# Second attention of a two-layer kernel: keys from the back, maxima two units ahead, causal masks on Pool

## What is computed

```
q, k, v = split(x @ w_qkv)            # x: layer norm of the residual; B=2, S=1024, D=128
q, k = rope(q), rope(k)               # H=16 heads, dh=8
scores = einsum('bhqd,bhkd->bhqk', q, k) * dh ** -0.5
scores = where(tril, scores, -huge)   # causal
attn = softmax(scores)
out = einsum('bhqk,bhkd->bhqd', attn, v) @ w_out
```

## Time and profile before

| | |
|---|---|
| median of 3 runs | 993.67 us (993.42 to 994.7) |
| profiled execution | 993.18 us |
| its span, first to last instruction | 991.3 us |
| busy over the span: PE, PEld | 849.9 (86%), 505.0 (51%) |
| busy: DVE, ACT, POOL | 595.4 (60%), 516.4 (52%), 329.3 (33%) |
| mean granted clock of TensorE | 0.92 |
| second attention, first scores to last values | 621.4 to 938.5 |

### The profile page before, as it was taken

One profiled execution on the slowest core, in us unless ns is written; L12 is line 12 of the kernel. 1 busy time (PEld: TensorE's weight loads), 2 busy tenths in 40 slices (PEclk: granted clock), 3 DMA queues, 4 the chain that ended last, 5 costly groups with the idle time before them and its releaser, 6 DMA issues.

```text
span 991.3 us, 15069 instructions
## 1 busy us (share of the span) xinstructions
PE 849.9 (86%) x5146; PEld 505.0 (51%) x5146; DVE 595.4 (60%) x1294; ACT 516.4 (52%) x875; POOL 329.3 (33%) x332
## 2 busy tenths in 40 slices
PE   5899999988999865899998435899999999999858
PEld 2454444343343233479987323555555555555435
DVE  6867776767666157553357598557575575754051
ACT  3246566564565642336665211656656566565632
POOL 3327666655566861660140840110202102000000
PEclk9779999998999996799999566899999999999969
DMA  9300000000000000112230200000000000000001
GB/s 330 123 1 1 1 1 1 1 1 1 1 1 1 1 1 0 59 59 62 70 97 29 84 3 1 1 1 1 1 2 1 1 0 0 0 1 1 1 1 43
DMA packets 22634, 24.38 MB, mean 25 GB/s; under 512 B 3591, under 2 KB 20105, under 8 KB 22314
## 3 DMA queue, kind: packets, MB, share of 16 engines
q1 hardware_dynamic: 19896, 17.90, 5.5%
q0 software_dynamic: 2048, 4.20, 1.5%
q10 hardware_dynamic: 626, 1.43, 0.4%
HBM read 14.34 MB, written 9.18 MB: 24 GB/s over the span
## 4 chain that ended last, share of the span: by engine, by line
PE 62%; DVE 23%; ACT 7%; issue 5%; POOL 2%; DMA 1%; ACTq 0%; DVEq 0%; SPq 0%; POOLq 0%
PE ps L1348 8%; PE ps L1400 6%; PE ps L1032 6%; PE ps L1024 5%; PE ps L1001 5%; DVE mx_part L2021 5%; PE ps L1374 4%; DVE mx_part L1631 3%; ACT rounded L613 3%; PE ps L1040 3%; PE ps L1291 3%; DVE cT L1654 2%; PE ps L990 2%; PE ps L1202 2%; ACT pt L851 2%
## 5 line engine op out<-in xcount | busy, mean ns | idle before, releaser
L1631 DVE TENSOR_REDUCE mx_part<-ps 128x1 f32<-128x512 f32 x256 | 162.5, 681 | 70.6 <-PE ps L1001 69.8
L851 ACT ACTIVATE pt<-ps 128x1024 f32<-128x1024 f32 (+1 forms) x160 | 142.8, 938 | 86.7 <-PE ps L1374 45.7
L670 ACT ACTIVATE pt<-ps 128x512 f32<-128x512 f32 x256 | 139.9, 596 | 80.3 <-PE ps L1024 78.2
L2021 DVE TENSOR_REDUCE mx_part<-ps 128x1 f32<-128x512 f32 (+3 forms) x256 | 138.9, 586 | 37.7 <-PE ps L1352 23.9
L1348 PE MATMUL ps<-rounded 128*128 128x512 f32 (+3 forms) x384 | 143.1, 426 | 12.2 <-DVE mx_part L2021 4.5
L613 ACT ACTIVATE rounded<-ps 32x512 fp32r<-32x512 f32 (+3 forms) x166 | 98.2, 593 | 100.9 <-PE ps L1327 32.2
L1024 PE MATMUL ps<-rounded 100*128 100x512 f32 x256 | 121.0, 484 | 8.5 <-ACT pt L670 7.8
L1001 PE MATMUL ps<-rounded 98*128 98x512 f32 x256 | 107.9, 444 | 17.4 <-DVE mx_part L1631 16.7
L1348 PEld LDWEIGHTS ps<-rounded 128*128 128x128 f32 x384 | 73.7, 203 | 76.2 <-DVE mx_part L2021 49.8
L1374 PE MATMUL ps<-rounded 128*128 128x512 f32 (+3 forms) x384 | 104.2, 370 | 8.9 <-ACT pt L851 7.2
L2021 DVE TENSOR_REDUCE mx<-ps 128x1 f32<-128x128 f32 (+3 forms) x128 | 57.2, 487 | 83.4 <-PE ps L1352 82.0
(11 more groups left out here) (249 smaller groups left out, 1285.9 us busy)
## 6 DMA issues: line engine op xcount, KB each, us to landing
wm<-in_wm SPq DMA_DIRECT2D x1, 4896.0 KB, 15.5
kstage<-to_experts SPq DMA_DIRECT2D x10, 256.0 KB, 3.4
of_experts<-pt SPq DMA_DIRECT2D x10, 256.0 KB, 2.3
to_experts<-kstage SPq DMA_DIRECT2D x4, 512.0 KB, 4.1
wm<-in_experts SPq DMA_DIRECT2D x1, 1028.0 KB
x<-in_x SPq DMA_DIRECT2D x4, 256.0 KB, 6.2
out<-x SPq DMA_DIRECT2D x4, 256.0 KB, 2.3
to_experts<-kstage SPq DMA_DIRECT2D x2, 448.0 KB, 4.4
```

Source lines behind the costliest of these rows:

```text
L670: nc.scalar.activation(pt0(k, i), ps[:, ST0_BANKS[i % 2], :], ACT.Exp, scale=SCALE0).then_inc(exp_done, 1)
L851: nc.scalar.activation(pt[:, 4 * (t % 2) + 2 * g:4 * (t % 2) + 2 * g + 2, 0:w], ps[:, ST1_BANKS[2 * g]:ST1_BANKS[2 * g] + 2, 0:w], ACT.Exp ...
L1631: v.tensor_reduce(mx_part[u % 2][:, o:o + 1], ps[:, max_bank(u, n), :], AX_X, ALU.max).then_inc(max_done, 1)
L2021: v.tensor_reduce(dst, ps[:, banks[s % len(banks)], o:o + w], AX_X, ALU.max).then_inc(max1_done, 1)
```

## The change

It touches the second attention only.

- **Order of keys and queries.** `ST1` now begins with the second half of the queries, and goes through the keys from the back: steps 0 to 2 are the diagonal tiles of the second half (4; 5 with 7; 6), steps 3 to 6 key tiles 3 to 0, steps 7 to 9 the diagonal tiles of the first half (0; 1 with 3; 2). The halves of a stack that are used up first are so free first.
- **Maxima.** `MX1` goes head by head, starts with the tiles of queries and keys of the second half, and the tiles run `MX1_AHEAD = 8` further ahead: in every step of unit `u` there are four, one behind the scores of each head; the last eight, in steps 8 and 9, belong to unit `u + 2`. Eight tiles of unit 1 come ahead of unit 0's first scores. The split of the maxima comes after step 7.
- **Stacks.** Keys are turned before queries, the second half before the first; ScalarE's four key copies are issued one by one between exponentials (`STACK1_KEYS`), and the counts of `stacked` follow (10 a unit). Turns: unit `u + 1`'s first halves in steps 0 and 2, unit `u + 2`'s second halves in steps 3 and 7, maxima both in step 9, contexts in steps 2 and 8, each turn in the middle of a step or at its end.
- **Masks.** The 32 bf16 matmuls a unit on the key-side scores go, and `mask_kq` with its load. Pool applies `affine_select` in place to the exponentials in `pt`: one instruction for each diagonal block of 128 keys and 128 queries over the 4 heads, 8 a unit. The values of a diagonal step wait for `masked1` in place of the exponentials.
- **Pool.** `stage` is cut in keys, queries and values; in each unit Pool stages the keys of `u + 2`, masks steps 0 to 2, stages the queries of `u + 2` and the values of `u + 1`, and masks steps 7 to 9.
- **Values.** The last values of a unit move behind step 0's scores of the next one.
- **Loops.** All eight units are straight code on every engine.

```diff
 ST1 = []
-for c in range(S // CH):
+for c in reversed(range(S // CH)):
     j0 = c * TC
-    ST1 += [(c, ((j, 0, CH),)) for j in range(j0 + 1)]
-    ST1 += [(c, ((j0 + 1, 0, CH - P), (j0 + 3, CH - P, P))), (c, ((j0 + 2, 0, CH - 2 * P),))]
+    own = [(c, ((j0, 0, CH),)), (c, ((j0 + 1, 0, CH - P), (j0 + 3, CH - P, P))), (c, ((j0 + 2, 0, CH - 2 * P),))]
+    ST1 += own + [(c, ((j, 0, CH),)) for j in reversed(range(j0))]
+DIAG1 = [[(o, w) for j, o, w in parts if j >= c * TC] for c, parts in ST1]
...
-for i0, c in ((0, 0), (TC, 0), (TC, 1)):
+for i0, c in ((TC, 1), (TC, 0), (0, 0)):
...
-    MX1 += [(r, c, p) for p in parts for r in range(HG)]
+    MX1 += [(r, c, p) for r in range(HG) for p in parts]
...
-MX1_STEP = (5, 5, 5, 5, 5, 5, 5, 5, 0, 0)
+MX1_AHEAD = 2 * HG
+MX1_SPLIT_STEP = K1 - 2
+NSTACK1 = 2 * (HG + 1)
+STACK1_KEYS = {0: (1, 1, 0), 1: (1, 1, 2), 4: (2, 0, 0), 5: (2, 0, 2)}
...
+            def mask(u, k):
+                if DIAG1[k]:
+                    pool.wait_ge(exp1_done, u * (2 * K1) + (2 * k + 2))
+                for o, w in DIAG1[k]:
+                    block = pt[:, 4 * (k % 2):4 * (k % 2) + HG, o:o + P]
+                    nc.gpsimd.affine_select(block, block, [[0, HG], [1, P]], ALU.is_ge, 0.0, base=0,
+                                            channel_multiplier=-1).then_inc(masked1, 1)
...
-            with pool.Fori(1, U1 // 2) as i:
-                for pp in range(2):
-                    stage(i * 2 + pp, pp, True)
+            for u in range(U1):
+                if u + 2 < U1:
...
+                    stage_keys(u + 2, u % 2)
+                for k in range(K1_FIRST):
+                    mask(u, k)
+                if u + 2 < U1:
+                    stage_queries(u + 2, u % 2)
+                if u and u + 1 < U1:
+                    stage_values(u + 1, 1 - u % 2)
+                for k in range(K1_FIRST, K1):
+                    mask(u, k)
...
             def unit1(u, pp, first=False, s=True, t=True):
                 for k in range(K1):
-                    exps1(u, k, first)
+                    for g in range(2):
+                        exps1(u, k, g, first)
+                        if k in STACK1_KEYS:
+                            du, n, r = STACK1_KEYS[k]
+                            if u + du < U1:
+                                stack_keys(u + du, (u + du) % 2, n, r + g)
+                        if k == 2 and g == 0 and s:
+                            stack_queries(u + 1, 1 - pp, 1)
+                        if k == 7 and g == 0 and t:
+                            stack_queries(u + 2, pp, 0)
+                        if k == K1 - 1 and s:
+                            max_rows1(u + 1, 1 - pp, g)
+                    if k == 0 and not first:
+                        context1_T(u - 1, 1)
                     if k == K1_FIRST:
-                        context1_T(u, 0, first)
+                        context1_T(u, 0)
...
                 elif not first:
-                    pe.wait_ge(max1_done, u * NMX1)
+                    pe.wait_ge(max1_done, (u - 1) * NMX1 + MX1_END[s - len(banks)])
...
-            def masks1(t):
-
-                c, parts = ST1[t]
-                if parts[0][0] < c * TC:
-                    return
-                for r in range(HG):
-                    for j, o, w in parts:
-                        ins = mm(ps[:, ST1_BANKS[r], o:o + P], identb[:], mask_kq[:], start=False,
-                                 stop=(o == parts[-1][1]))
-                    if r % 2:
-                        ins.then_inc(st1_mm, 1)
...
-                pe.wait_ge(exp1_done, u * (2 * K1) + (2 * t + 2))
+                if DIAG1[t]:
+                    pe.wait_ge(masked1, u * NDIAG1 + DIAG1_UPTO[t])
+                else:
+                    pe.wait_ge(exp1_done, u * (2 * K1) + (2 * t + 2))
...
                 for k in range(K1):
...
+                    for r in range(HG):
+                        scores1(u, pp, r, k, first)
+                        piece(k, r)
+                        if r != 1:
+                            continue
+                        if k == 0 and s:
+                            turn_stack(u + 1, 1 - pp, 2, (m1_rows, u * 2 + 2))
+                        if k == 2 and s:
+                            turn_stack(u + 1, 1 - pp, 3, (stacked, (u + 1) * NSTACK1 + (2 * HG + 1)))
+                        if k == 7 and t:
+                            turn_stack(u + 2, pp, 1, (stacked, (u + 2) * NSTACK1 + HG))
+                        if k == K1 - 1 and s:
+                            turn_max1(u + 1, 1 - pp, 0, (ctx1_out, u * 4 + 2))
                     if k:
                         values1(u, pp, k - 1, first)
...
+                    elif u:
+                        values1(u - 1, 1 - pp, K1 - 1, u == 1)
+                    if k == 2 and u:
+                        turn_context1(u - 1, 1, (stacked, (u + 2) * NSTACK1) if s else (m1_rows, u * 2 + 2))
+                    if k == 3 and t:
+                        turn_stack(u + 2, pp, 0, (ctx1_out, u * 4) if u else (stacked, (u + 2) * NSTACK1))
+                    if k == K1 - 2:
+                        turn_context1(u, 0, (stacked, (u + 2) * NSTACK1 + (HG + 1)) if t else (ctx1_out, u * 4))
+                    if k == K1 - 1 and s:
+                        turn_max1(u + 1, 1 - pp, 1, (m1_rows, u * 2 + 3))
...
+                if n == len(MX1) - 3:
+                    turn_stack(1, 1, 0, (qk_out, NT))
+            turn_max1(0, 0, 0, (stacked, NSTACK1 + HG))
+            turn_stack(1, 1, 1, (m1_rows, 1))
+            turn_max1(0, 0, 1, (stacked, NSTACK1 + (HG + 1)))
+            for n in range(MX1_AHEAD):
+                scores_max1(1, 1, n)
+            for u in range(U1):
+                unit1(u, u % 2, first=(u == 0), s=(u + 1 < U1), t=(u + 2 < U1))
+            values1(U1 - 1, (U1 - 1) % 2, K1 - 1, False)
```

More of the change, by code:

```diff
@@ L576, in stage, with stage_values @@
+            def stage_values(u, pp):
+                if u >= 2:
                     pool.wait_ge(pv1_mm, u * K1 - K1)
@@ L855, in context1_T, with stack_queries @@
-            def context1_T(u, c, first):
-                act.wait_ge(pv1_mm, u * K1 + (K1_FIRST if c == 0 else K1))
-                if not first:
-                    act.wait_ge(ctx1_turn, u * 2 + (c - 1))
-                copy(cT[:, c, :], ps[:, CTX_BANK, :]).then_inc(ctx1_T, 1)
+            def stack_queries(u, pp, n):
+                act.wait_ge(stack_turn, u * 4 + (2 * n + 2))
+                cols = slice((1 - n) * CH, (2 - n) * CH)
+                copy(query_stack1[pp][:, cols], ps[:, TURN1_BANK, :]).then_inc(stacked, 1)
@@ new lines, in stack_keys, with max_rows1 @@
+            def stack_keys(u, pp, n, r):
+                act.wait_ge(stack_turn, u * 4 + (2 * n + 1))
+                cols, rows = slice((1 - n) * CH, (2 - n) * CH), slice(RS * r, RS * (r + 1))
+                copy(key_stack1[pp][rows, r, cols], ps[rows, TURN1_BANK, :]).then_inc(stacked, 1)
+            def max_rows1(u, pp, n):
+                act.wait_ge(m1_turn, u * 2 + (n + 1))
+                copy(query_stack1[pp][:, (1 - n) * CH:(2 - n) * CH], ps[:, TURN1_BANK, :]).then_inc(m1_rows, 1)
@@ new lines, in exps1 @@
+            def exps1(u, t, g, first):
+                w = sum(m for _, _, m in ST1[t][1])
+                act.wait_ge(st1_mm, u * (2 * K1) + (2 * t + g + 1))
+                if not (first and t < 2):
+                    act.wait_ge(pv1_mm, u * K1 + (t - 1))
+                nc.scalar.activation(pt[:, 4 * (t % 2) + 2 * g:4 * (t % 2) + 2 * g + 2, 0:w],
+                                     ps[:, ST1_BANKS[2 * g]:ST1_BANKS[2 * g] + 2, 0:w], ACT.Exp,
+                                     scale=SCALE1).then_inc(exp1_done, 1)
@@ L880, in _ @@
                     front_qkv(c, t)
-            for hf in range(2):
-                max_rows1(0, 0, hf)
             act.wait_ge(keys_zero[1], 1)
-            for n in range(2):
-                stack(1, 1, n)
-            unit1(0, 0, first=True)
-            unit1(1, 1)
-            with act.Fori(1, U1 // 2 - 1) as i:
-                unit1(i * 2, 0)
-                unit1(i * 2 + 1, 1)
-            unit1(U1 - 2, 0, t=False)
-            unit1(U1 - 1, 1, s=False, t=False)
+            for r in range(HG):
+                stack_keys(1, 1, 0, r)
+            max_rows1(0, 0, 0)
+            stack_queries(1, 1, 0)
+            max_rows1(0, 0, 1)
+            for u in range(U1):
+                unit1(u, u % 2, first=(u == 0), s=(u + 1 < U1), t=(u + 2 < U1))
+            context1_T(U1 - 1, 1)
             for c in range(NCH):
@@ L1394, in values1 @@
                     pe.wait_ge(v_copied, u + 1)
-                if parts[0][0] == 0 and not (first and c == 0):
-                    pe.wait_ge(ctx1_T, u * 2 + c)
-                pe.wait_ge(exp1_done, u * (2 * K1) + (2 * t + 2))
+                if t == K1_FIRST or t == 0 and u:
+                    pe.wait_ge(ctx1_T, u * 2 + (1 - c))
+                if DIAG1[t]:
```

(25 more changed lines are left out.)

226 lines of the change are left out of this document (96 added, 130 removed).

## The result

The changed kernel takes 960.88 us (median of 4 runs, 958.83 to 964.08), the kernel before 993.54 (4 runs, 993.18 to 994.7): a ratio of 0.9672, 95% interval 0.9644 to 0.97. It is faster, by 32.7 us, where 23.0 were forecast. The profiled execution took 961.01 with a span of 959.2; that of before had a span of 991.3.

What follows compares the result with a forecast made beforehand. TensorE bounds the second attention, losing time to a two-bank ping-pong with VectorE. Gains of 2.3 (unit 0), 15.5 (units 1 to 5), 4.4 (unit 6) and 0.8 (unit 7) sum to 23.0: forecast 970.7 us, range 952 to 986.

Steps and rivals of the forecast that it cites:

- likeliest case: Whole kernel: the forecast itself, 970.7 us, with 965 to 977 counted as its case; chance 0.42.
- TensorE nearly full: Rival, second attention: first maximum overlaps better, loss only 4.3 a unit, unit 36.5, total 958 us; chance 0.20.
- Masks off TensorE: Each unit of the second attention: 32 key-side mask matmuls go, saving 1.5 us of TensorE's own time.
- A mask of 0.80: Pool, second attention: one mask block takes 0.80 us at the copy's rate for 512 elements, bounds 0.40 and 1.28.
- The loss of 6.0 a unit: Steady unit: TensorE loses 6.0 us beside own work of 32.3; unit 38.2, gain 3.1; loss before 7.5.
- Spread, stacks and maxima ahead: Steady unit: four tiles every step, earlier split and covered copies, all within the loss falling from 7.5 to 6.0 us.
- Unit 0: Start of second attention: scores at about 625.3, unit takes 38.2 less 0.9 plus 1.2, ends 663.8 not 666.13; gain 2.3 us.
- Unit 6: Second attention: lacks eight tiles (3.1) and two turns (0.7), waits 0.6 for a mask; 35.0 not 39.4, gain 4.4 us.
- Unit 7: Last unit, ScalarE's: loop through Pool's mask longer in diagonal steps, mask matmuls ahead of exponentials go; net gain 0.8 us.
- The slow mask: Rival: Pool's mask blocks delay values; slower than before from 1.65 us a block, 1028 us at 2.56; chance 0.12.
- Nothing overlooked: Denies the rival that wait order or straight-code delivery eats the gain, 0 to 10 us slower than before; chance 0.08.
- 0.4 for one instruction of the split: VectorE's split of maxima: one two-input instruction per unit could meet a Pool mask, costing 0.4 us that VectorE can spare.

Runs made afterwards that it cites:

- no_mask: Changed kernel without any key-side causal mask, values waiting for exponentials alone: 1000.6 us where the kernel before took 1033.74; steady unit 37.12, as in the changed kernel.
- pe_masks: Changed kernel with key-side masks back on TensorE, right behind each head's scores: ratio 0.983 to the kernel before; steady unit 39.05 us against 37.12.
- both_undone: Changed kernel with key-side masks on TensorE and maxima tiles five each in steps 0 to 7, none ahead of unit 0: 984.48 us, unit 40.74.
- mask_slow: Changed kernel with one clearing of an unused tile before each Pool mask, making a block 1.19 us: 1013.76 us, before 1033.74 there; unit 37.75.
- mask_slower: Changed kernel with two clearings of an unused tile before each Pool mask, making a block 1.86 us: 1031.66 us; unit 41.20 against 37.12.
- gaps: Changed kernel with each step's tiles 0 and 1 ahead of their scores, 2 and 3 behind: ratio 0.9664 to the kernel before; unit 36.77 us.

## Why the prediction was right, and where its sizes were off

The sign and the mechanism held: TensorE bound before and binds after, it gained by fewer matmuls and fewer waits for VectorE, and the mask lies beside it. The median of 960.9 is in the range of 952 to 986, but under the 965 to 977 of the likeliest case, and nearer to the rival "TensorE nearly full" (958) than to the forecast of 970.7; so is the unit, 37.1 beside 36.5 and 38.2. By its own steps:

- **Masks off TensorE, 1.5 a unit.** The mechanism was right; putting them back costs 1.9, since more than the masks' own pitches is lost.
- **A mask of 0.80.** It took 0.63. The copy's rate was an upper estimate, not a middle one. The margin of 1.8 was read rightly (1.87), and with no_mask the cover is shown. By the margin, an estimate from (1.87 - 0.1) / 2, a block of up to 0.9 costs a steady unit nothing.
- **The loss of 6.0 a unit.** This is the mis-sized term: own work of 32.3 and a unit of 37.12 leave 4.8. The gain of a steady unit is so 4.1 and not 3.1, and five of them make 5.2 of the 9.1 us that the sum fell short. By the prediction's own count per step, steps 1 to 4 (740.28 to 754.62) lost 2.6, where 3.4 stood. The full step shown lost 0.65, as VectorE started 0.43 after the matmul and not 0.5, and for the stack in step 2 TensorE waited 0.20 and not 0.4. The six other steps lost 2.3, where 2.6 stood. "TensorE nearly full" had 4.3 for the whole term and was nearer.
- **Spread, stacks and maxima ahead.** The prediction took the loss down from 7.5 to 6.0, and named a cover of 1.1 at the unit's boundary as a part of that; so it left 0.4 for the spread. The runs turn this around: the spread is worth 1.8, and all that is neither mask nor spread 0.54. So two errors that partly cancel stand behind the size of this term, and that it came out within 1.2 is in part luck.
- **Unit 0, 2.3.** The first scores came at 624.27 (forecast 625.3), the unit took 38.42 (38.5). The start, 1.0 earlier than forecast, is what the sum was short by.
- **Unit 6, 4.4.** 5.05: the same tiles' loss. The wait of 0.6 for a mask did not show; TensorE waited 0.53 for VectorE's context there instead.
- **Unit 7, 0.8.** It gained 2.3, and not by the step named. The prediction weighed mask matmuls that go against a longer loop through Pool and came to a net gain. The runs make it even: with the masks on TensorE the unit takes 24.5 (pe_masks), on Pool 24.4, with none 22.8 (no_mask). The 2.2 are there in both_undone too (24.5 against 26.7 before), so they belong to what that run keeps; which part of it is open. The price of 6 us per us of mask was high as well: mask_slow takes 26.9, 4.5 per us between a block of 0.63 and one of 1.19. Its diagonal values do wait for Pool, as forecast, on TensorE's timeline of the changed kernel:

```profile
888.99 1.05 PE L1425 MATMUL ps<-pt,v_cur 128*9 128x384 f32 x16 [0.79 <-POOL pt L597]
...
905.53 1.55 PE L1425 MATMUL ps<-pt,v_cur 128*9 128x384 f32 x24 [0.71 <-POOL pt L597]
```

- **The slow mask.** The rival's form was right: mask_slow cost what the margin says. In mask_slower its price was too low, as it left out the clock, but since the gain to eat was 32 and not 23, the break-even moved from 1.65 to some 1.8 to 1.9. Nothing like 12 cycles an element is in the 0.63 of a block of 512 (the Trainium skill, "GPSIMD Engine Reference", section 3.1, gives that for data-dependent branching): the select does not have that price. Its 1.2 ns an element lies between the 1.0 of the memset (0.63 for 640 columns, in mask_slow) and the 1.6 of the copy.
- **Nothing overlooked** in the order of waits: unit 1 and unit 3 are 37.11 and 37.12, and the second chip repeats 37.13.

What stays open: which part of the rest gave unit 0 and unit 7 their 2.2 us each in both_undone. The 0.65 behind the second attention needs no cause: over the fourteen traces, with the same code there, this stretch lies between 51.6 and 52.8.

## What to carry to other kernels

Where two engines hand two buffers to and fro, write down when each buffer is taken and freed in one step, for every kind of step, and place the filling engine's longest piece of other work right behind the filling of both. Work taken off the bound engine is free on an idle one exactly as long as it fits into the margin between its producer and its consumer: read that margin from the trace of before, and price what lies above it at one for one (mask_slow), and at more where the wait grows long enough to lower TensorE's clock (mask_slower). After each reordering look for the wait that comes up next; here the wait for one copy held back half of what the new order gave, until the turn was moved too.

## What the runs showed of the hardware

**The clock fell after a wait of 1.9 us.** In mask_slower TensorE waited 1.88 us and then ran at a granted clock of 0.55 over 2.60 us, mostly at the 1.2 GHz level, and at 1.00 (2.4 GHz) both ahead of it and from 797.00 on. Waits of 0.79 in the same place in unit 7 of the changed kernel, and of 0.67 in step 8 of the same unit of mask_slower, left the clock at 1.00. So 1.9 us of wait cost 1.9 + 1.5.

**A small VectorE instruction that starts beside a select lasts until the select ends.** VectorE's timeline of the changed kernel, the split of the maxima, with the mask of Pool that runs beside it:

```profile
765.68 0.18 DVE L2053 TENSOR_TENSOR mx<-mx_part 128x16 f32<-128x16 f32 x1
765.89 0.52 DVE L2058 TENSOR_SCALAR qstage<-mx 128x32 fp32r<-128x32 f32 x1
766.44 0.22 DVE L2060 SCALAR_TENSOR_TENSOR qstage<-mx,qstage 128x32 fp32r<-128x32 f32 x1
```

```profile
765.72 0.64 POOL L597 TENSOR_SCALAR_AFFINE_SELECT pt<-pt 128x512 f32<-128x512 f32 x1 [15.54 <-ACT pt L882]
```

The second instruction ends at 766.41, just after the select (766.36), and took 0.20 in before. It is so in the six of the changed kernel's eight splits in which it starts during a select (0.52 to 0.54); in the two others, and in all of no_mask, which has no selects, it took 0.20. The first instruction, which has two inputs and began 0.04 ahead of the select, was not held up. In the split of unit 7's maxima it began 0.23 behind the start of one (Pool's select from 876.50 to 877.13), and there it was:

```profile
876.73 0.43 DVE L2053 TENSOR_TENSOR mx<-mx_part 128x16 f32<-128x16 f32 x1
```

In gaps the select starts just ahead of the third instruction, which has two inputs as well, and that one takes 0.66 to 0.67 in six splits, against 0.22. Beside a memset, which has no input (mask_slower), the two with two inputs keep their 0.18 and 0.22, and the one with one input still takes 0.50 to 0.52 in six of eight. The prediction's 0.4 for one instruction of the split was thus about right in size (0.3), but hit mostly another of its instructions than one with two inputs; the Trainium skill, "SBUF — State Buffer", section "Who interferes with whom", does list this form among those that can take the shared ports.
